# Experts: the second matrices are split in their own expert's opening step, and the sums of weight quarters move into the delta turns

## The chip, the cores and the metric

One core of a Trainium2 chip runs the whole program. The metric is the device time of one execution in microseconds. The kernel is written by hand: every engine has its own instruction stream, and semaphores alone order the streams.

## The reference, cut to what matters

The program is a stack of four layers on 4096 tokens of 256 values. The change touches the second layer, a mixture of eight experts, and the copies of weights that the fourth layer reads much later.

```python
# layer 2, on z = layernorm(x), after a delta-rule attention (layer 1)
probs = softmax(z @ w_router); weights = top-2 of probs, as a mask over 8 experts
h   = gelu(z @ w1[e] + b1[e])          # 256 -> 1024, for every expert e
out = sum over e of weights[:, e] * (h @ w2[e] + b2[e])   # 1024 -> 256
x   = x + out
# layer 4 has two 1024x1024 matrices, h1 and h2; the kernel multiplies them by blocks
# with seven products in place of eight, from sums of 512x512 quarters of each matrix
```

## The kernel before, in words

**The delta turns.** Layer 1 works through the 4096 tokens in 16 turns of two chunks (`TURNS`). Behind the turns, in pieces spread over them, follow the residual sum (x1), the layernorm z1 of it, the router and, for each block of four chunks, the place of every token in its two experts' lists. GpSimd (POOL) has three jobs here. For each chunk of a turn it multiplies one tile (L384) and issues the load of a word block `ckb` (L373), which VectorE folds into `lowb` (L622). Between turns it issues the scatters of z1 rows into `z1_by_expert` (L344): 64 indirect DMAs in all, eight to each block, half a block per pass of its loop over `u`. The order of that loop is written out by hand: `turn(u + 1)` first, then the scatters of pass u. The last six scatters stand in the next program block (L1529).

SyncE (SP) stores the finished tokens of each block (L294) and, behind the first five stores, issues 14 copies of weight quarters from the input to `hidden_weight_blocks` (L297), 1024 KB each, three to a block. These are the first terms of the sums that layer 4 needs. At the end SP loads the first expert's matrices (L313, L314).

**The experts.** The tokens of an expert are worked on in tiles of 256 (`TT`); this input gives 35 tiles. A step has TensorE (PE) make the up product of tile t (`up`, L1468 to L1470 through the helper `mm3`), transpose the rows of the next tile (L1597), and make the down product of the tile before (`down`). ScalarE (ACT) takes each of eight up results from its PSUM bank with the gelu (L1666); four banks are used in turn, so PE can be four of them ahead. VectorE (DVE) splits h into a high and a low part (L1760, L1762), adds the bias to the down result (`y`, L1728), and ACT multiplies it by the gate (`gated`, L1655) before POOL adds the rows to the tokens in DRAM (L1542).

Every product is made of three in a rounded format, so each weight matrix is needed as a high part (ACT, `high_part`, L1658) and a low part (DVE, `low_part`, L1743), and there are two buffers of either. The step that opens an expert (`before < e`) makes the up product of its first tile and the down product of the last tile of the expert before. In that step ACT makes the high part of the next expert's first matrix, waits for the end of the down product (`dn_ps`) and makes the high part of the next expert's second matrix; only then comes `gated`. DVE makes the low part of the next first matrix ahead of `y`, and that of the next second matrix at the end of the step. SP loads both raw matrices two experts ahead (`weights`, L1495, L1496).

**The sums of quarters** are made by POOL in the experts' openings (`hidden_sums`, L1551): 16 DMAs of 512 KB with `accum_op=add` into `hidden_weight_blocks`, two behind the token additions of each of the openings 1 to 5 and three in each of 6 and 7. In opening 7 POOL goes on with two multiplications of the next layer's weights (L1534).

Of the kernel before, what the change touches and what calls it, by code (L numbers as in the profile page):

```python
# [16 lines left out]
S, D, DS, HID, NE = 4096, 256, 64, 1024, 8  # L17
# [11 lines left out]
NP7 = 7  # L29
# [47 lines left out]
def build(nc, A):  # L77
# [5 lines left out]
    with ctx:  # L83
# [4 lines left out]
        first_sems = []  # L88
# [171 lines left out]
        hw_cp, hw_add = sem("hidden_blocks_copied"), sem("hidden_blocks_summed")  # L260
        first_terms = ((W_A11, 0, 0), (W_A12, 0, 1), (W_A22, 1, 1), (W_S3, 0, 0), (W_S1, 1, 1), (W_S2, 0, 0), (W_S4, 0, 1))
        ew_ld, v_ld = sem("expert_weights_loaded"), sem("vectors_loaded")
        nw_ld = [sem(f"next_weights_loaded_{q}") for q in range(2)]
        x_rdy, lq_rdy, mk_cp = sem1("right_side_ready"), sem1("decayed_q_ready"), sem1("decay_rows_ready")
        mk_rdy, mk_ps, mk_out = sem1("masks_ready"), sem1("mask_transposes_in_psum"), sem1("masks_taken")

# [9 lines left out]
        @block.sync  # L276
        def _(sp):
            for n in range(XL):
                cs = slice(XP[n], XP[n + 1])
                sp.dma_start(x_tok[:, cs, :], x_tok_d[:, cs, :]).then_inc(ld_x[n], 16)  # L280
            sp.dma_start(vec[:, 0:11, :], A["vectors"].rearrange("p (n k) -> p n k", k=KT)).then_inc(v_ld, 16)
            sp.wait_ge(nu_out, NB)
            kept = ((0, 2 * D * HID), (WORDS - D * HID, WORDS))
            for lo, hi in kept:
                sp.dma_start(raw_d[lo:hi], A["ffn"][lo:hi]).then_inc(bulk, 16)
            sp.wait_ge(consts, 2)
            for d_, a0, a1 in fills:
                v = d_.rearrange("(a p r) d -> a p (r d)", p=128, r=4)
                for a in range(a0, a1):
                    sp.dma_start(v[a], zero[:, 0:v.shape[2]]).then_inc(bulk, 16)  # L290

            def store_tokens(b):
                sp.wait_ge(x1_rdy, 2 * b + 2)
                sp.dma_start(x2_blocks[b], x_tok[:, b * CPB:(b + 1) * CPB, :]).then_inc(x1_st, 16)  # L294

            def first_term(layer, i, out_half, in_half):
                sp.dma_start(hw_rows[layer * NP7 + i], quarter(layer, out_half, in_half)).then_inc(hw_cp, 16)  # L297

            terms = [(layer, *term) for term in first_terms for layer in range(2)]
            for b in range(NB - 3):  # L300
                store_tokens(b)
                for term in terms[3 * b:3 * b + 3]:
                    first_term(*term)
            free = x_tok[:, :, :].rearrange("p c d -> p (c d)")
            sp.wait_ge(x1_st, 16 * (NB - 3))
            sp.wait_ge(z1_rdy, 2 * (NB - 4))
            sp.dma_start(free[:, 0:KT * HID].rearrange("p (k n) -> p k n", k=KT),
                         A["w1"].rearrange("e (k p) n -> e p k n", p=128)[1]).then_inc(nw_ld[1], 16)
            sp.dma_start(free[:, KT * HID:KT * HID + HID // 128 * D].rearrange("p (k n) -> p k n", n=D),
                         A["w2"].rearrange("e (k p) n -> e p k n", p=128)[1]).then_inc(nw_ld[1], 16)  # L310
            store_tokens(NB - 3)
            sp.wait_ge(pp_ps, NC)
            sp.dma_start(st1[:, :, :], A["w1"].rearrange("e (k p) n -> e p k n", p=128)[0]).then_inc(ew_ld, 16)  # L313
            sp.dma_start(st2[:, :, :], A["w2"].rearrange("e (k p) n -> e p k n", p=128)[0]).then_inc(ew_ld, 16)  # L314
            for b in range(NB - 2, NB):
                store_tokens(b)
# [31 lines left out]
        def _(pool):  # L348
# [29 lines left out]
            def turn(t):  # L378
                for j in range(2):
# [6 lines left out]
                    if c + 2 < NC:  # L386
                        load_words(c + 2, j)

            turn(0)
            for u in range(2 * NB + 5):  # L390
                if u + 1 < TURNS:
                    turn(u + 1)
                b = block_of(u, 1, 7)
                if b == 0:
                    pool.wait_ge(bulk, BULK)
                if b is not None:
                    scatter(pool, b, 0, CPB)
                b = block_of(u, 0, 8)
                if b is not None and b < NB - 1:
                    scatter(pool, b, CPB, 2 * CPB)  # L400
# [1040 lines left out]

        def landed(e):

            return nw_ld[e % 2], 32 * ((e + 1) // 2)


        ptwo = ctx.enter_context(ExitStack())
# [40 lines left out]
        def _(sp):  # L1488
            sp.dma_start(b1s[:, :], A["b1T"]).then_inc(eb_ld, 16)

            def weights(e):
                if e >= 2:
                    sp.wait_ge(ew_rdy, e - 1)
                    sp.wait_ge(w2_rdy, e - 1)
                sp.dma_start(raw1[e % 2][:, :, :], w1_d[e]).then_inc(nw_ld[e % 2], 16)  # L1495
                sp.dma_start(raw2[e % 2][:, :, :], w2_d[e]).then_inc(nw_ld[e % 2], 16)  # L1496

            def rows(e, t0, i):
                sp.wait_ge(xt_ps, t0 + i + 1)
# [5 lines left out]
            for e in range(NE):  # L1505
                t0 = sp.value_load(tiles0[0:1, e:e + 1], min_val=MIN_TILES * e, max_val=MT - MIN_TILES * (NE - e))
                own = sp.value_load(own0[0:1, e:e + 1], min_val=MIN_TILES, max_val=S // TT)
                rows(e, t0, 0)
                if e == 0:
                    for n in range(NE):  # L1510
                        sp.dma_start(b2s[:, n, :], A["b2"][n:n + 1, :].broadcast_to([128, D])).then_inc(b2_ld, 16)
                    sp.wait_ge(x1_st, 16 * NB)
                if 1 <= e < NE - 2:
                    weights(e + 2)
                if e == 2:
                    sp.dma_start(wst, A["W_tm"].rearrange("(k p) n -> p k n", p=128)).then_inc(wt_ld, 16)
                    sp.dma_start(tmr_, A["tm"].rearrange("(o n) -> o n", o=1).broadcast_to([128, 3 * D])).then_inc(wt_ld, 16)
                with sp.Fori(1, own) as i:
                    rows(e, t0, i)
            total = tile_count(sp)  # L1520

            sp.wait_ge(xt_ps, total + 1)
# [3 lines left out]
        def _(pool):  # L1526
# [15 lines left out]
                    pool.indirect_dma_start(x2_d, bass.IndirectOffsetOnAxis(to_row[:, j:j + 1].bitcast(u32), 0), yg[:, j, :], None,  # L1542
                                            compute_op=ALU.add).then_inc(y_out, 16)

            def hidden_sums(n):

                def add(layer, to, half, more=None):
                    base = layer * NP7
                    source = quarter(layer, 1, 0) if more is None else hw_rows[base + more]
                    k = 2 * half  # L1550
                    pool.dma_start(hw_rows[base + to][:, k:k + 2, :], source[:, k:k + 2, :], accum_op=ALU.add).then_inc(hw_add, 16)  # L1551

                if n == 0:
                    pool.wait_ge(hw_cp, 16 * 2 * NP7)
                for half in range(2):
                    if n < 4:
                        add(n % 2, (W_S3, W_S1)[n // 2], half)
                    elif n < 6:
                        pool.wait_ge(hw_add, 16 * 8)
                        add(n % 2, W_S2, half, W_S1)  # L1560
                if n == 5:
                    pool.wait_ge(hw_add, 16 * 10)
                    add(0, W_S4, 0, W_S2)
                if n == 6:
                    pool.wait_ge(hw_add, 16 * 13)
                    add(0, W_S4, 1, W_S2)
                    for half in range(2):
                        add(1, W_S4, half, W_S2)

            def step(e, t, before, start):  # L1570
                add_to_tokens(t)
                if before < e and e >= 1:
                    hidden_sums(e - 1)
                if before < e and e == NE - 1:
                    time_mix_weights()

# [63 lines left out]
        @block.scalar  # L1640
        def _(act):
            act.sem_inc(h_act, 4)
            for done in first_sems:
                act.sem_clear(done)
            act.wait_ge(ew_ld, 32)
            for st_, w in ((st1, w1s[0]), (st2, w2s[0])):
                nc.scalar.activation(w[0][:, :, :], st_[:, :, :], ACT.Copy).then_inc(wh_rdy, 1)
# [12 lines left out]
            def step(e, t, before, start):  # L1660
                ahead = before < e and e + 1 < NE
                for m in range(KH):
# [5 lines left out]
                    if start and m == 5:  # L1668
                        act.wait_ge(ew_rdy, 1)
                        act.wait_ge(w2_rdy, 1)  # L1670
                        act.dma_start(st1[:, :, :], w1_d[2]).then_inc(nw_ld[0], 16)
                        act.dma_start(st2[:, :, :], w2_d[2]).then_inc(nw_ld[0], 16)
                if ahead:
                    act.wait_ge(*landed(e + 1))
                    high_part(w1s, raw1, e + 1)
                    act.wait_ge(dn_ps, t * 2 + 2)
                    high_part(w2s, raw2, e + 1)
                if not start:
                    gated(t)

# [9 lines left out]
        def _(dve):  # L1690
# [54 lines left out]
            def step(e, t, before, start):  # L1745
# [3 lines left out]
                for m in range(0, KH, 2):  # L1749
                    i = m // 2  # L1750
                    dve.wait_ge(h_act, t * KH + (m + 2 + 4))
                    if i < 3:
                        dve.wait_ge(hs_free, t * 3 + (i + 1))
                    else:
                        if ahead:
                            low_part(w1s, raw1, e + 1, 2 * e + 3, ew_rdy)
                        if not start:
                            y(before, t)
                        dve.wait_ge(dn_ps, t * 2 + 2)
                    V.tensor_copy(hs[0][:, m:m + 2, :], h32[:, m:m + 2, :]).then_inc(h_st, 1)  # L1760
                    dve.wait_ge(h_st, t * 4 + (i + 1))
# [2 lines left out]
                rows_of_tokens(t)  # L1764
                hand_on(t)
                if ahead:
                    low_part(w2s, raw2, e + 1, 2 * e + 4, w2_rdy)

            rows_split(0)
            dve.wait_ge(wh_rdy, 2)  # L1770
# [1669 lines left out]
```

## Time and profile before

| what | value |
|---|---|
| median of 3 runs | 2003.12 us (1997.04 to 2003.94) |
| profiled execution | 2002.26 us, of which the span from first to last instruction is 2000.2 us |
| mean granted TensorE clock | 0.957 of full |
| TensorE matmul busy | 1826.2 us (91%) |
| VectorE busy | 1479.8 us (74%) |
| ScalarE busy | 1113.1 us (56%) |
| GpSimd busy | 308.5 us (15%) |

The program has stages with different limits, so the shares above say little about one of them. Times in the views are microseconds from the start of the span. The delta turns end at about 463 us, the rest of the router's work to 516 us, the experts from 523 to 953 us, and the two last layers behind that.

### The profile page before, as it was taken

The page shows a single profiled execution, that of the slowest core. Times are in us where ns is not written, and L with a number is a line of the kernel's source. Part 1 is how long each engine was busy: PE and PEld are TensorE (multiplying, and loading weights), DVE is VectorE, ACT ScalarE, POOL GpSimd, SP SyncE. Part 2 cuts the span into 40 slices and gives each one's busy share as a digit, 9 for nine tenths or more (in the row PEclk, how much of TensorE's full clock was granted, in tenths as well). Part 3 has the DMA queues.
Part 4 walks back from the last instruction along what each step waited for, and adds up shares of the span by engine and source line. Part 5 has one row for each costly group of instructions (what it writes and reads, how often), then busy time and mean ns, then how long its engine had stood idle before and what let it go on. Part 6 is the DMA issues. An engine that isn't in the chain of part 4 may idle for free. (4 is left out here: it accounts for less than half of the span.)

```text
span 2000.2 us, 31208 instructions
## 1 busy us (share of the span) xinstructions
PE 1826.2 (91%) x10840; PEld 1561.7 (78%) x10840; DVE 1479.8 (74%) x2966; ACT 1113.1 (56%) x1987; POOL 308.5 (15%) x282
## 2 busy tenths in 40 slices
PE   7999999997499999999577769899999999999999
PEld 5688888886499999999455547677788888888887
DVE  7567888887576676666599889888776776776675
ACT  3656666663344443442688867664556456456454
POOL 0000012224333322333100011111000000000000
PEclk9999999996699999999888879999999999999999
DMA  3099334423446545344444553333343143142141
GB/s 110 29 393 405 128 120 141 142 92 117 128 96 136 112 88 111 64 75 69 128 112 87 108 128 136 144 126 127 116 142 132 54 176 128 56 176 106 58 174 64
DMA packets 107986, 251.79 MB, mean 126 GB/s; under 512 B 8992, under 2 KB 51616, under 8 KB 99616
## 3 DMA queue, kind: packets, MB, share of 16 engines
q1 hardware_dynamic: 82288, 201.16, 28.6%
q0 software_dynamic: 23680, 46.28, 12.6%
q10 hardware_dynamic: 1888, 2.67, 0.4%
q8 instruction: 75, 1.23, 0.3%
q14 instruction: 55, 0.45, 0.1%
HBM read 172.88 MB, written 107.61 MB: 140 GB/s over the span
## 5 line engine op out<-in xcount | busy, mean ns | idle before, releaser
L1542 POOL DMA_INDIRECT tokens_behind_spare_rows<-yg,row_of_token x70 | 119.1, 1701 | 294.9 <-DVE row_of_token L1733 273.2
L1666 ACT ACTIVATE h<-bank,b1s 128x256 f32<-128x256 f32 x280 | 123.6, 471 | 35.0 <-PE bank L1470 20.3
L3177 ACT ACTIVATE hidden_quarter<-hidden_quarter,scl 128x512 f32<-128x512 f32 x96 | 67.6, 721 | 118.8 <-DVE hidden_quarter L3013 118.7
L1655 ACT ACTIVATE yg<-yt,own_gates 128x256 f32<-128x256 f32 x68 | 31.0, 502 | 183.3 <-DVE yt L1728 176.9
L1223 PE MATMUL bank<-st,L 128*128 128x128 f32 x768 | 117.4, 279 | 13.2 <-DVE st L573 13.1
L957 ACT ACTIVATE L<-bank 128x512 f32<-128x512 f32 x128 | 75.1, 593 | 94.6 <-PE bank L1215 94.3
L2398 PE MATMUL bank<-split_0h,hidden_weights 128*128 128x512 f32 x320 | 126.5, 395 | 0.0
L2398 PE MATMUL bank<-split_1h,hidden_weights 128*128 128x512 f32 x320 | 125.4, 392 | 0.1
L2399 PE MATMUL bank<-split_0l,hidden_weights 128*128 128x512 f32 x320 | 125.3, 391 | 0.0
L2399 PE MATMUL bank<-split_1l,hidden_weights 128*128 128x512 f32 x320 | 125.3, 391 | 0.0
L1215 PE MATMUL bank<-L 128*128 128x128 f32 x640 | 119.3, 276 | 0.0
L1223 PEld LDWEIGHTS bank<-st,L 128*128 128x128 f32 x768 | 100.6, 193 | 17.7 <-DVE st L573 7.0
L573 DVE TENSOR_TENSOR st<-st,bank 128x256 f32<-128x256 f32 x192 | 75.0, 416 | 53.0 <-PE bank L1223 52.2
L1214 PE MATMUL bank<-L 128*128 128x128 f32 x512 | 101.4, 280 | 0.7
L2398 PE MATMUL bank<-split_2h,hidden_weights 128*128 128x512 f32 x256 | 101.4, 396 | 0.0
L1762 DVE TENSOR_TENSOR hsl<-h,hsh 128x512 fp32r<-128x512 f32 x140 | 96.9, 692 | 4.8
L2399 PE MATMUL bank<-split_2l,hidden_weights 128*128 128x512 f32 x256 | 100.2, 391 | 0.0
L1215 PEld LDWEIGHTS bank<-L 128*128 128x128 f32 x640 | 95.5, 194 | 0.0
L2965 DVE SCALAR_TENSOR_TENSOR hidden_quarter<-bank,scl,x_tok 128x512 f32<-128x512 f32 x64 | 47.4, 748 | 55.8 <-ACT x_tok L3140 55.8
L1468 PE MATMUL bank<-xTh,w_1h 128*128 128x256 f32 x288 | 81.2, 282 | 7.2 <-ACT h L1666 7.2
L2972 DVE TENSOR_TENSOR split_2l<-hidden_quarter,split_2h 128x1024 fp32r<-128x1024 f32 x48 | 59.1, 1251 | 35.4 <-ACT split_2h L3159 35.4
L1214 PEld LDWEIGHTS bank<-L 128*128 128x128 f32 x512 | 79.3, 194 | 7.2 <-issue 2.7
(488 smaller groups left out, 6013.6 us busy)
## 6 DMA issues: line engine op xcount, KB each, us to landing
hidden_weights<-hidden_weight_blocks SPq DMA_DIRECT2D x64, 1024.0 KB, 4.8
z_by_expert<-zero SPq DMA_DIRECT2D x64, 520.0 KB, 15.6
hidden_weight_blocks<-in_ffn_dram SPq DMA_DIRECT2D x14, 1024.0 KB, 9.8
ckb<-in_ffn_dram POOLq DMA_DIRECT2D x32, 352.0 KB, 5.0
xg<-z_by_expert SPq DMA_DIRECT2D x36, 260.0 KB, 3.2
x_tok<-in_w_dram SPq DMA_DIRECT2D x8, 1024.0 KB, 8.8
x_tok<-x_T SPq DMA_DIRECT2D x16, 512.0 KB, 6.1
x_tok<-after_time_mix SPq DMA_DIRECT2D x15, 512.0 KB, 8.8
```

What stands on the lines that cost most here:

```text
L573: V.tensor_tensor(z_ if SQUARES <= n < LEVELS - 1 else x_, x_, B[2 + j][:, 0:256], ALU.subtract if n == 0 else ALU.add).then_inc(ap_rdy, 1)
L957: A_.activation(L[:, p, j, (n + 1) % 2, :, :], src, ACT.Copy).then_inc(sq_cp, 1)
L1214: T.matmul(B[j][:, 256 * m:256 * m + 128], b_, a, start=True, stop=True)
L1215: last = T.matmul(B[j][:, 256 * m + 128:256 * m + 256], a, b_, start=True, stop=True)
L1223: last = T.matmul(B[2 + j][:, 0:256].rearrange("p (a m d) -> p a m d", a=2, m=2)[:, :, m, :], Ln[:, 2 * m + 1, :], right, start=True, stop ...
L1468: nc.tensor.matmul(out, a[0], b[0], start=first, stop=False)
L1542: pool.indirect_dma_start(x2_d, bass.IndirectOffsetOnAxis(to_row[:, j:j + 1].bitcast(u32), 0), yg[:, j, :], None, compute_op=ALU.add).then ...
L1666: nc.scalar.activation(h32[:, m, :], B[m % 4][:, 0:TT], ACT.Gelu_apprx_tanh, bias=b1s[:, e * KH + m:e * KH + m + 1]).then_inc(h_act, 1)
L1762: V.tensor_tensor(hs[1][:, m:m + 2, :], h32[:, m:m + 2, :], f32(hs[0][:, m:m + 2, :]), ALU.subtract).then_inc(h_rdy, 1)
L2398: nc.tensor.matmul(out, w, x[0], start=first, stop=False, **more)
L2399: return nc.tensor.matmul(out, w, x[1], start=False, stop=last, **more)
L3177: A_.activation(QB[to][:, m, :], src, ACT.Gelu, scale=scl[:, off[lay.name] + row:off[lay.name] + row + 1]).then_inc(g_act, 1)
```

## The change

Five edits, as the diff has them:

1. The second matrix of expert e is split in opening e and no longer in opening e-1 (ACT `high_part(w2s, raw2, e)` ahead of that of the next first matrix, no wait for `dn_ps`; DVE `low_part(w2s, ...)` behind `y`). The low part of the next first matrix goes to the end of DVE's step.
2. So `y` stands ahead of both low parts in an opening.
3. The raw second matrices get semaphores of their own, and SP loads them one expert later than the first matrices.
4. `hidden_sums` leaves the experts. It becomes four groups of four DMAs in POOL's passes u = 12 to 15 of the delta turns, each between `turn(u + 1)` and the pass's scatters. The first group waits for all 14 copies, each later one for the landing of all the groups before it. SP issues the copies five to a block instead of three.
5. The clearing of the first stage's semaphores goes from the start of ACT's expert program to the end of SP's loops.

```diff
@@ first program block, SP @@
-                for term in terms[3 * b:3 * b + 3]:
+                for term in terms[5 * b:5 * b + 5]:
                     first_term(*term)
...
-                         A["w2"].rearrange("e (k p) n -> e p k n", p=128)[1]).then_inc(nw_ld[1], 16)
+                         A["w2"].rearrange("e (k p) n -> e p k n", p=128)[1]).then_inc(nd_ld[1], 16)
@@ first program block, POOL @@
+            def hidden_sums(n):
+                if n == 0:
+                    pool.wait_ge(hw_cp, 16 * 2 * NP7)
+                else:
+                    pool.wait_ge(hw_add, 16 * 4 * n)
+                to, more = ((W_S3, None), (W_S1, None), (W_S2, W_S1), (W_S4, W_S2))[n]
+                for layer in range(2):
+                    source = quarter(layer, 1, 0) if more is None else hw_rows[layer * NP7 + more]
+                    for k in (0, 2):
+                        pool.dma_start(hw_rows[layer * NP7 + to][:, k:k + 2, :], source[:, k:k + 2, :],
+                                       accum_op=ALU.add).then_inc(hw_add, 16)
+
             turn(0)
             for u in range(2 * NB + 5):
                 if u + 1 < TURNS:
                     turn(u + 1)
+                if 0 <= u - (TURNS - 4) < 4:
+                    hidden_sums(u - (TURNS - 4))
@@ experts, SP @@
-            def weights(e):
-                if e >= 2:
-                    sp.wait_ge(ew_rdy, e - 1)
-                    sp.wait_ge(w2_rdy, e - 1)
+            def up_weights(e):
+                sp.wait_ge(ew_rdy, e - 1)
                 sp.dma_start(raw1[e % 2][:, :, :], w1_d[e]).then_inc(nw_ld[e % 2], 16)
-                sp.dma_start(raw2[e % 2][:, :, :], w2_d[e]).then_inc(nw_ld[e % 2], 16)
+
+            def down_weights(e):
+                sp.wait_ge(w2_rdy, e - 1)
+                sp.dma_start(raw2[e % 2][:, :, :], w2_d[e]).then_inc(nd_ld[e % 2], 16)
...
+                if 2 <= e < NE - 1:
+                    down_weights(e + 1)
                 if 1 <= e < NE - 2:
-                    weights(e + 2)
+                    up_weights(e + 2)
...
+            for done in first_sems:
+                sp.sem_clear(done)
@@ experts, POOL @@
-            def hidden_sums(n):
...
             def step(e, t, before, start):
                 add_to_tokens(t)
-                if before < e and e >= 1:
-                    hidden_sums(e - 1)
                 if before < e and e == NE - 1:
                     time_mix_weights()
@@ experts, ACT @@
             act.sem_inc(h_act, 4)
-            for done in first_sems:
-                act.sem_clear(done)
...
+                if before < e and e >= 1:
+                    act.wait_ge(*down_landed(e))
+                    high_part(w2s, raw2, e)
                 if ahead:
                     act.wait_ge(*landed(e + 1))
                     high_part(w1s, raw1, e + 1)
-                    act.wait_ge(dn_ps, t * 2 + 2)
-                    high_part(w2s, raw2, e + 1)
                 if not start:
                     gated(t)
@@ experts, DVE @@
                     else:
-                        if ahead:
-                            low_part(w1s, raw1, e + 1, 2 * e + 3, ew_rdy)
                         if not start:
                             y(before, t)
+                        if before < e and e >= 1:
+                            low_part(w2s, raw2, e, 2 * e + 2, w2_rdy)
                         dve.wait_ge(dn_ps, t * 2 + 2)
...
                 hand_on(t)
                 if ahead:
-                    low_part(w2s, raw2, e + 1, 2 * e + 4, w2_rdy)
+                    low_part(w1s, raw1, e + 1, 2 * e + 3, ew_rdy)
```

## Rows read from the trace of the kernel before

**Rows 1.** The page: TensorE's busy tenths and clock, 40 slices of 50 us

```profile
PE   7999999997499999999577769899999999999999
...
PEclk9999999996699999999888879999999999999999
```

**Rows 2.** Waits, 490 to 965 us: us in total, times, longest

```profile
PE bank L1597 <- DMA xg<-z_by_expert: 19.6, 2, 19.2
...
PE bank L1468 <- ACT h L1666: 12.1, 8, 3.2
```

**Rows 3.** Timeline of PE after gaps: start, us, line, tile, count, idle before

```profile
523.05 1.12 PE L1597 MATMUL bank<-ident,xg 128*128 128x128 f32 x4 [19.20 <-DMA xg<-z_by_expert]
...
552.32 0.38 PE L1468 MATMUL bank<-xTh,w_0h 128*128 128x256 f32 x1 [0.88 <-ACT h L1666]
588.75 0.38 PE L1468 MATMUL bank<-xTh,w_1h 128*128 128x256 f32 x1 [1.34 <-ACT h L1666]
...
924.48 0.58 PE L1468 MATMUL bank<-xTh,w_1h 128*128 128x256 f32 x1 [3.16 <-ACT h L1666]
```

**Rows 4.** Timeline of ACT in expert 1's opening

```profile
584.71 1.93 ACT L1658 ACTIVATE w_0h<-st 128x2048 fp32r<-128x2048 f32 x1 [3.80 <-PE bank L1470]
587.43 0.91 ACT L1655 ACTIVATE yg<-yt,own_gates 128x256 f32<-128x256 f32 x2 [0.80 <-DVE yt L1728]
```

**Rows 5.** Timeline of DVE in the same opening

```profile
584.37 2.28 DVE L1743 TENSOR_TENSOR w_0l<-st,w_0h 128x2048 fp32r<-128x2048 f32 x1
586.57 0.75 DVE L1728 TENSOR_TENSOR yt<-bank,b2s 128x256 f32<-128x256 f32 x2
...
588.64 2.28 DVE L1743 TENSOR_TENSOR w_0l<-st,w_0h 128x2048 fp32r<-128x2048 f32 x1
```

**Rows 6.** Timelines of POOL and DVE in expert 7's opening

```profile
914.04 5.18 POOL L1534 TENSOR_TENSOR x_tok<-x_tok 128x768 f32<-128x768 f32 x2
...
915.08 4.45 DVE L1760 CAST hsh<-h 128x512 fp32r<-128x512 f32 x1
```

**Rows 7.** Timeline of POOL around the last delta turns

```profile
415.86 0.58 POOL L373 DMA_DIRECT2D ckb<-in_ffn_dram  x1 [16.15 <-DVE lowb L622]
...
440.11 0.58 POOL L373 DMA_DIRECT2D ckb<-in_ffn_dram  x1 [16.26 <-DVE lowb L622]
441.00 1.02 POOL L344 DMA_INDIRECT z_by_expert<-Z,slotz  x1 [0.30 <-issue]
...
463.53 0.97 POOL L344 DMA_INDIRECT z_by_expert<-Z,slotz  x1 [0.30 <-issue]
483.00 0.97 POOL L344 DMA_INDIRECT z_by_expert<-Z,slotz  x1 [18.49 <-DVE slotz L733]
...
516.27 0.97 POOL L344 DMA_INDIRECT z_by_expert<-Z,slotz  x1 [0.30 <-issue]
```

**Rows 8.** Sums by line, openings 1 and 6: duration (ns), start, landing

```profile
L1551 POOL DMA_DIRECT2D hidden_weight_blocks<-in_ffn_dram x2: 1955/2152/2348, 593.6 to 594.4; - x2
DMA to landing us min/median/max: 8.8/9.7/10.5
...
L1551 POOL DMA_DIRECT2D hidden_weight_blocks<-hidden_weight_blocks x3: 1481/1752/2199, 868.0 to 869.2; - x3
DMA to landing us min/median/max: 7.7/10.0/13.8
```

**Rows 9.** Stretches: busy us of PE, PEld, DVE, ACT, POOL; clock, DMA share, GB/s

```profile
868.00:884.00 16.00, 16.00 (x140) 16.00 (x140) 11.10 (x27) 4.44 (x10) 6.55 (x6) 1.00 0.98 159
...
426.00:440.00 14.00, 13.00 (x112) 12.19 (x108) 11.10 (x37) 8.69 (x25) 0.00 (x0) 1.00 0.11 39
...
471.00:480.00 9.00, 3.43 (x14) 2.42 (x14) 8.27 (x26) 2.58 (x5) 0.00 (x0) 0.50 0.88 291
```

**Rows 10.** Timelines of DVE and of PE in the last delta turn

```profile
442.85 0.88 DVE L622 TENSOR_TENSOR lowb<-lowb,ckb 128x704 int32<-128x704 int32 x1
...
463.72 0.77 PE L1247 MATMUL bank<-state,st 128*128 128x128 f32 x2 [1.07 <-DVE Wb L580]
```

More of the change, by code:

```diff
@@ L262, in build @@
         ew_ld, v_ld = sem("expert_weights_loaded"), sem("vectors_loaded")
-        nw_ld = [sem(f"next_weights_loaded_{q}") for q in range(2)]
+        nw_ld = [sem(f"next_up_weights_loaded_{q}") for q in range(2)]
+        nd_ld = [sem(f"next_down_weights_loaded_{q}") for q in range(2)]
         x_rdy, lq_rdy, mk_cp = sem1("right_side_ready"), sem1("decayed_q_ready"), sem1("decay_rows_ready")
@@ L1442, in landed, with down_landed @@
         def landed(e):
-            return nw_ld[e % 2], 32 * ((e + 1) // 2)
+            return nw_ld[e % 2], 16 * ((e + 1) // 2)
+        def down_landed(e):
+            return nd_ld[e % 2], 16 * ((e + 1) // 2)
         ptwo = ctx.enter_context(ExitStack())
@@ L1543, in add_to_tokens @@
                                             compute_op=ALU.add).then_inc(y_out, 16)
-            def hidden_sums(n):
[L1547 to L1568, printed above, removed]
             def step(e, t, before, start):
                 add_to_tokens(t)
-                if before < e and e >= 1:
-                    hidden_sums(e - 1)
                 if before < e and e == NE - 1:
@@ L1671, in step @@
                         act.dma_start(st1[:, :, :], w1_d[2]).then_inc(nw_ld[0], 16)
-                        act.dma_start(st2[:, :, :], w2_d[2]).then_inc(nw_ld[0], 16)
+                        act.dma_start(st2[:, :, :], w2_d[2]).then_inc(nd_ld[0], 16)
+                if before < e and e >= 1:
+                    act.wait_ge(*down_landed(e))
+                    high_part(w2s, raw2, e)
                 if ahead:
```

## The prediction

> **What bounds the kernel now.** I read the page's slices first. In the experts (slices 10 to 18) PE is busy all the time, and the clock is full after the start; ahead of them stands a stretch with PE at 4 tenths and a lower clock [rows 1]. The reader should take from this that the experts are bound by PE, so that an edit there is worth only the holes in PE's time, and that the way into the experts is bound by something else. The waits of the window name both: PE waits 19.2 us at once for the rows of the first tile, and 12.1 us in 8 pieces for the gelu to free a bank [rows 2]. PE's own timeline puts the pieces in their places [rows 3]: 0.88 us behind the first step, 1.34 us behind opening 1 (and 1.34 or 1.35 behind each of openings 2 to 6: six holes), and 3.16 us behind opening 7.
>
> **Why the holes are there.** In opening 1 the down product ends by 584.7. Only then does ACT make the high part of the second matrix, 1.93 us, and it waits 0.80 more for the bias addition [rows 4]; DVE is in a low part of 2.28 us from 584.37, so its addition starts at 586.57 instead of 584.7 [rows 5]. The gating comes 2 us late, the gelu behind it too, and PE, four banks ahead, runs out of banks. In opening 7 there is nothing to split. There a cast of DVE takes 4.45 us, and it ends only after POOL's two multiplications [rows 6].
>
> **What bounds the way in.** POOL's timeline [rows 7]: scatters follow one another every 1.275 us (0.97 busy, 0.30 idle). There are 8 to each block; three eights stand between 483.00 and the last one at 516.27, which waited for no places. The idle time of 18.49 us ahead of 483.00 is POOL's slack. PE begins at 523.05, 6.8 us after the last scatter's start [rows 3, 7]: the scatter, its landing and the load of the rows. Every microsecond by which the last scatter is late is paid in full.
>
> **The change part by part.** The sum stands against the profiled execution, 2002.26 us (span 2000.2 and 2.1 around it); the median of the runs is 0.9 above that.
>
> *Splits and bias addition in the opening.* The work is the same: 7 high parts of 1.93 and 7 low parts of 2.28 [rows 4, 5], one opening later. In openings 1 to 6 ACT now makes two high parts behind the eighth gelu, which ended 3.80 + 1.93 us ahead of 584.71 [rows 4]: from 579.0 to 582.9, before the down product ends. The addition starts at 584.7, the gating ends some 2 us after that, and a bank is free when PE wants it, as in any other tile. That takes away 6 x 1.34 = 8.0. The first step loses one high and one low part, and with them its 0.88. What is late next is DVE: behind the addition come 2.28, a cast and subtraction, and 2.28 again, which makes 584.7 + 0.75 + 2.28 + 1.1 + 0.3 + 2.28 = 591.4. PE came to a stop at 588.75 - 1.34 = 587.4, in the middle of an up product begun at 584.5 [rows 3], so without the stop it has the next rows transposed by 590.8; DVE's lateness runs down over the next tile's splits, and its addition is some 0.5 us late, of which I let PE pay 0.15. Six times, that is 0.9. The down product of the second tile needs the low part at about 590; it is made at 587.7. **Experts: -8.0.**
>
> *Opening 7.* It gains a high and a low part, both behind what PE waits for. POOL no longer has three sums ahead of its multiplications, so these come 1.7 us earlier and meet the tile's first DVE instructions instead of the cast. The lock-out lasts 5.2 us either way [rows 6]; I take 0, with bounds of -1 and +1.
>
> *Loads.* SP has one wait split in two; each second matrix is issued an expert ahead of its use, at least two tiles of 11.6 us or so (two halves of an up product are 5.8 and a down product as long), and even the 512 KB sums land in 8 to 14 [rows 8]. What is queued behind the new waits are the rows of the expert's second tile; both semaphores were raised an opening before, so 0. *Semaphore clearing* leaves ACT's start, where the path is the scatters', and goes to SP's end, ahead of a load that waits for PE anyway: 0. *Copies five to a block*: 14 copies by the third block, into DMA engines that stand at 0.11 in a quiet stretch [rows 9]; word blocks are loaded most of a turn ahead; SP only waits for x1 behind them: 0, with an upper bound of 1.
>
> *The sums in POOL's passes.* First their price. Two sums issued 0.8 us apart land within 0.8 + 10.5 = 11.3 us; three in opening 6 within 1.2 + 13.8 = 15.0, where two of that kind took 10.5, so a further one costs 4.5 [rows 8]. Four are 11.3 + 9.0 = 20.3 us for a group from the input, 19.5 for one inside the copy. During them the DMA engines are full (share 0.98), at 159 GB/s [rows 9]: they are bound by the engines, and nothing says they would be faster elsewhere. The issues of three take 1.2 us from the first start to the last and up to 2.2 for the last [rows 8], so 1.1 each, and 4.5 for four.
>
> By the Trainium skill, "DMA: Bandwidth & Descriptors", section "Anatomy of one DMA — SWDGE (gpsimd) path", such a transfer takes about 2.0 us and its bytes at 436 GB/s; that would be some 7 us for four (an estimate by that page), and the groups would not wait for each other. Its fit says nothing of accumulation, and the landings above disagree with it.
>
> Now the chain on POOL:
> - Group 0 follows the word block of 415.86 [rows 7], at 416.7, and lands at 437. The next word block is issued behind it and behind four scatters, at 416.7 + 4.5 + 5.1 + 0.5 = 427, and must be there at 442.85 [rows 10]; it comes behind the group and the scatters in the queue, at about 440. 0, at worst 3.
> - Group 1 follows the word block of 440.11, at 441.0 [rows 7], and lands at 441.0 + 20.3 + 1 for that block = 462.3. The half block of scatters behind it and the last two multiplications of the turns end at 441.0 + 4.5 + 5.1 + 1 = 452; PE wants these at 463.7 [rows 10]. 0.
> - Group 2 must wait for group 1: 462.3. Alone it would land at 481.8. But from 471 to 480 SP loads the first expert's 2 MB and stores a block, a share of 0.88 over 9 us, 7.9 us of all engines [rows 9]. Full engines mean the two add up: 489.7.
> - Group 3 waits for that: 489.7, and is issued by 494.2. Behind it stand the scatters of blocks 4 to 7, 32 in all, 31 x 1.275 = 39.5: the last starts at 533.7, and not at 516.3 [rows 7]. The last block had its places without a wait by then [rows 7], so nothing else is later than POOL.
>
> **Way into the experts: +17.4**, between +9.5 (the loads overlap with group 2 at no cost: 481.8) and, with 5.2 us a further sum, the word block late by 3 and a queue that holds scatters up, about +28.
>
> For the adding up of group 2 and the loads there is a rule beside the rows: the same page, section "Queues, rings and completion order", says that each DMA engine takes the queues in turn, packet by packet. By it the engines do both works one after the other, as taken above.
>
> *Sum.* 2002.3 - 8.0 + 17.4 = **2011.7, say 2011**, 8 above the median of the runs. About 0.5%, or 10 us, is what a measurement of this kernel can tell from no change, so this is on the slow side of no change, and near the edge.
>
> **The rivals.**
> - *Slower: POOL's chain is longer than worked out.* Place: group 3 and the 32 scatters behind it. Price: from 4.5 to 5.2 us for a further sum in four groups, of which three are on the chain, +4 to +6, and the queue's hold on the scatters while group 3 lands (until about 510), a few more: +25 in all, and 2019. It decides against me when group 3 is issued later than 492. For it: every small delay on the chain adds to the others. Against it: in opening 6 three sums were taken by the queue at once [rows 8].
> - *Faster: the sums are not the price.* By the page's figure, or if the quiet DMA engines of these turns do four sums in under 10 us, group 2 is done at 462 and group 3 at 472, the scatters of 483 are on time, and only -8.0 is left: 1994. For it: POOL's slack of 18.49 us. Against: landings and share [rows 8, 9].
> - *The holes stay.* If DVE's double load in the opening makes the next tile late by as much as was gained, the change does not do what it says, and only +17.4 stands: 2019.7. Against it: the addition is first in line when the down product ends.
> - *The loads cost group 2 nothing*: -8.0 + 9.5, 2004.
>
> **How the numbers follow.** The forecast's own case, chain and gain as worked out, has 0.48 and a spread of some 4 us about 2011, from 2007 to 2015. The longer chain has 0.22 (2015 to 2024), the holes that stay 0.06, the free loads 0.14 (2001 to 2007), cheap sums 0.10 (1993 to 1996). Left out of the range are cheap sums and the far end of the longer chain. Range 1999 to 2022. Against the median of 2003.1 the edges of no change are 1993 and 2013. Slower takes a third of the first case (0.16) and all of the next two (0.28): 0.44. Faster has 0.05: half of the cheap sums. The same: 0.51.
>
> **What would show it.** Right: the pieces of 1.34 us behind openings 1 to 6 are gone from PE's timeline; the wait of PE for the first rows is about 36 us and not 19.2, and PE begins the experts at about 540; POOL has no slack ahead of its last 32 scatters; one issue of group 2 comes at about 462, one of group 3 at about 490; the expert stage from its first to its last product is 8 us shorter. Wrong: group 3 issued before 476, so that POOL catches up; or a hole of DVE's making in the second tile of each expert; or a wait for a word block at 443, which would move the turns themselves.

## The result and the profile after

The changed kernel takes 1992.25 us (median of 5 runs, 1989.26 to 1997.32) against 2003.94 us for the kernel before in the same session: a ratio of 0.9949 with a 95% interval of 0.9928 to 0.997. Timed twice more on other occasions it gave 0.9965 (0.9951 to 0.9979) and 0.9947 (0.993 to 0.9963). It is faster by about half a per cent, and the forecast was 0.4% slower. The profiled execution is 1992.25 us long, its span 1990.5.

PE's timeline of the changed kernel, the lines with idle time ahead of them, answers to [rows 2, 3]:

```profile
524.17 1.12 PE L1594 MATMUL bank<-ident,xg 128*128 128x128 f32 x4 [23.75 <-DMA xg<-z_by_expert]
526.95 0.57 PE L1487 MATMUL bank<-xTh,w_0h 128*128 128x256 f32 x1 [1.67 <-DVE xTl L1716]
537.18 0.38 PE L1487 MATMUL bank<-xTh,w_0h 128*128 128x256 f32 x1 [1.66 <-DVE xTl L1716]
543.70 0.66 PE L1594 MATMUL bank<-ident,xg 128*128 128x128 f32 x4 [0.81 <-DMA xg<-z_by_expert]
914.88 0.58 PE L1487 MATMUL bank<-xTh,w_1h 128*128 128x256 f32 x1 [2.96 <-ACT h L1661]
```

Between 543.70 and 914.88 no hole is left: the 0.88 and the six of 1.34 us are gone. The 2.96 us behind opening 7 are still there (3.16 before). The wait for the first rows is 23.75 us, not the 36 that were forecast.

POOL's timeline, in answer to [rows 7]: the word block that ends the last turn but one, the sums of group 1, of group 2 and of group 3, and the first and last scatter behind them.

```profile
438.59 0.58 POOL L374 DMA_DIRECT2D ckb<-in_ffn_dram  x1 [12.13 <-DVE lowb L637]
439.16 4.76 POOL L399 DMA_DIRECT2D hidden_weight_blocks<-in_ffn_dram  x4
...
456.81 3.50 POOL L399 DMA_DIRECT2D hidden_weight_blocks<-hidden_weight_blocks  x4 [6.71 <-DMA hidden_weight_blocks<-in_ffn_dram]
...
472.79 3.50 POOL L399 DMA_DIRECT2D hidden_weight_blocks<-hidden_weight_blocks  x4 [7.24 <-DMA hidden_weight_blocks<-hidden_weight_blocks]
...
476.59 1.04 POOL L345 DMA_INDIRECT z_by_expert<-Z,slotz  x1 [0.31 <-issue]
...
517.35 0.97 POOL L345 DMA_INDIRECT z_by_expert<-Z,slotz  x1 [0.30 <-issue]
```

The chain is the one forecast: POOL waits for group 1 and for group 2 (the two waits on a DMA), and from 476.59 on it has no slack. But group 3 comes at 472.8, where 489.7 was worked out.

**Where the 9.7 us of the two spans come from**, by the same event in both traces:

| event | before | changed | difference | of it in this stretch |
|---|---|---|---|---|
| PE's first instruction | 8.47 | 6.95 | -1.5 | -1.5 |
| SP's load of the first expert (end of the turns) | 471.13 | 467.05 | -4.1 | -2.6 |
| PE transposes the first rows | 523.05 | 524.17 | +1.1 | +5.2 |
| second step's first product | 536.27 | 537.18 | +0.9 | -0.2 |
| first product behind opening 7 | 924.48 | 914.88 | -9.6 | -10.5 |
| next layer's first transposes | 968.70 | 958.95 | -9.75 | -0.15 |

The first line is ahead of every edit. The second goes with the clock: PE's granted clock fell to half at about 463 us in the last turn of the kernel before, and at about 467 us in the changed one.

```profile
450.00:464.00 14.00, 11.52 (x96) 10.67 (x95) 11.50 (x41) 5.84 (x13) 9.26 (x10) 0.97 0.24 86
464.00:480.00 16.00, 9.88 (x39) 7.39 (x39) 12.11 (x46) 2.81 (x6) 0.50 (x1) 0.50 0.53 176
```

```profile
450.00:464.00 14.00, 11.57 (x98) 10.52 (x96) 11.41 (x42) 5.07 (x11) 6.38 (x8) 1.00 0.82 162
464.00:480.00 16.00, 7.97 (x36) 5.12 (x32) 14.07 (x60) 5.49 (x13) 7.55 (x9) 0.60 1.04 269
```

(Stretches of the kernel before, then of the changed one, columns as in [rows 9].) Another profiled execution of the same changed kernel began its first instruction at 8.41, had a mean clock of 0.78 from 460 to 465 us, and took 31.0 us from the word block to SP's load, where this one took 28.5 and the kernel before 31.0. So neither line belongs to the change. What is left to explain is the stretch on the way in, which costs, and the experts, which gain. The +5.2 of the third line is not all the change's: while POOL is the last to come, the 2.6 us by which the turns ended earlier are not used, and the chain itself adds the other 2.6.

### The profile page after: what moved, and what is told of

Same layout as the page of the kernel before. It is cut to its first block and busy times, and to the rows that moved or that the text cites. A ratio compares the mean times of both kernels' runs of the same rounds, so it can differ in the third digit from the quotient of the medians.

```text
span 1990.5 us, 31195 instructions
## 1 busy us (share of the span) xinstructions
PE 1821.0 (91%) x10840; PEld 1558.3 (78%) x10840; DVE 1476.9 (74%) x2966; ACT 1114.6 (56%) x1987; POOL 308.9 (16%) x282
## 5 line engine op out<-in xcount | busy, mean ns | idle before, releaser
L1712 DVE COPY raw_gates<-xg 128x8 f32<-128x8 f32 x36 | 8.0, 221 | 103.7 <-PE bank L1594 103.0
L1229 PEld LDWEIGHTS bank<-L 128*128 128x128 f32 x512 | 78.8, 193 | 7.3 <-issue 2.7
```

What stands on the lines that cost most here:

```text
L1229: T.matmul(B[j][:, 256 * m:256 * m + 128], b_, a, start=True, stop=True)
```

## The experiments

All kernels are compared by two stretches, which leave out the first accident and most of the second: **way in**, from the word block that ends the last turn but one to the last scatter (76.2 us before, 78.8 changed), and **experts**, from the second step's first product to the first one behind opening 7 (388.2 before, 377.7 changed). The way in isn't quite free of the clock. Where POOL has slack, it waits for the places that the turns deliver: one and the same kernel (early_apart and apart_again below) took 75.4 us with the turns' end 28.5 us behind the word block, and 76.8 us with 31.0. So differences of up to 1.4 us in the way in need not come from an edit.

**splits_only**: the changed kernel with the sums back in the openings.

```diff
-                if 0 <= u - (TURNS - 4) < 4:
-                    hidden_sums(u - (TURNS - 4))
...
-                for term in terms[5 * b:5 * b + 5]:
+                for term in terms[3 * b:3 * b + 3]:
...
                 add_to_tokens(t)
+                if before < e and e >= 1:
+                    hidden_sums(e - 1)
```

> The changed kernel with the sums of quarters back in the experts' openings and the copies three to a block: the edits of the splits alone. Theory A (the gain of the change is the closed holes of PE in the openings, and the sums play no part in the experts): from PE's first up product to the first product behind opening 7 the stage is as short as in the changed kernel, about 388 us and not 398.7; PE's holes behind openings 1 to 6 are gone; the way in is as in the kernel before, last scatter about 75 us after the first scatter of 441.0. Time some 10 us under the kernel before. Rival B (taking the sums out of the openings frees POOL and the DMA engines, and part of the gain comes from that): the expert stage gets back at least 3 us of its length, and holes or later bias additions are seen in openings with sums.

Measured: ratio 0.9969 (0.9958 to 0.9981). Way in 76.8 us, experts 380.7. So the splits alone are worth 7.5 us of the experts, and the sums' leaving is worth 3.0 more. Rival B has its part, and PE's timeline shows where:

```profile
877.35 0.38 PE L1473 MATMUL bank<-xTh,w_0h 128*128 128x256 f32 x1 [0.83 <-ACT h L1674]
917.64 0.58 PE L1473 MATMUL bank<-xTh,w_1h 128*128 128x256 f32 x1 [5.09 <-ACT h L1674]
```

Behind opening 6 a new hole of 0.83 us, and 5.09 in place of 2.96 behind opening 7. ACT's timeline names the first one's cause, and the landings of the token additions (issued from 860 to 872 us, splits_only, then the changed kernel) give its size:

```profile
876.03 0.91 ACT L1663 ACTIVATE yg<-yt,own_gates 128x256 f32<-128x256 f32 x2 [7.82 <-DMA tokens_behind_spare_rows<-yg,row_of_token]
...
DMA to landing us min/median/max: 4.2/9.3/9.3
```

```profile
DMA to landing us min/median/max: 3.7/3.8/4.4
```

The additions stand behind the three sums in POOL's queue and land after 9.3 us instead of 3.8; `gated` waits for them (`y_out`), and the gelu behind it. The second hole is the meeting of DVE and POOL in opening 7. Here two instructions of DVE are long and not one: a cast while POOL issues the sums, which ends at 907.45, and a subtraction across POOL's multiplications.

```profile
905.62 1.83 DVE L1769 CAST hsh<-h 128x512 fp32r<-128x512 f32 x1
907.48 5.64 DVE L1771 TENSOR_TENSOR hsl<-h,hsh 128x512 fp32r<-128x512 f32 x1
```

```profile
905.69 3.19 POOL L1561 DMA_DIRECT2D hidden_weight_blocks<-hidden_weight_blocks  x3
907.59 4.98 POOL L1544 TENSOR_TENSOR x_tok<-x_tok 128x768 f32<-128x768 f32 x2
```

Beside the 0.42 and 0.69 us that the two take elsewhere, DVE loses 6.36 us; in the changed kernel its one long cast (4.65 for 0.42) loses 4.23. The difference is 2.13, and so is that of the two holes (5.09 and 2.96).

**sums_only**: the kernel before with the sums moved (and the copies five to a block).

```diff
-                if before < e and e >= 1:
-                    hidden_sums(e - 1)
...
+                if 0 <= u - (TURNS - 4) < 4:
+                    hidden_sums(u - (TURNS - 4))
```

> The kernel before with the sums moved into passes 12 to 15 and the copies five to a block, and nothing else. Theory A: the six holes of 1.34 us stay, the expert stage keeps its 398.7 us, and the way in gets 2 to 4 us longer, because POOL waits for groups 1 and 2 (about 17 us a group) and then issues 32 scatters in a row. Time 1 to 5 us over the kernel before. Rival B: the expert stage is shorter by 3 us or more and the time is at or under that of the kernel before. My forecast's own price (20 us a group, 27 for the one beside the loads) would give 15 us more on the way in.

Measured: ratio 1.0004 (0.9992 to 1.0016). Way in 78.6 us, so +2.4 where the forecast had +17.4:

```profile
437.97 0.58 POOL L373 DMA_DIRECT2D ckb<-in_ffn_dram  x1 [12.14 <-DVE lowb L636]
...
471.63 3.49 POOL L398 DMA_DIRECT2D hidden_weight_blocks<-hidden_weight_blocks  x4 [7.76 <-DMA hidden_weight_blocks<-hidden_weight_blocks]
...
516.54 0.97 POOL L344 DMA_INDIRECT z_by_expert<-Z,slotz  x1 [0.30 <-issue]
```

Experts 387.6: the six holes of 1.34 stay, the first is 0.43 and that of opening 7 is 1.95. The sums' move alone is a little cost and a little gain, and the time cannot tell it from nothing.

**sums_early**: the groups three passes earlier, in 9 to 12.

```diff
-                if 0 <= u - (TURNS - 4) < 4:
-                    hidden_sums(u - (TURNS - 4))
+                if 0 <= u - (TURNS - 7) < 4:
+                    hidden_sums(u - (TURNS - 7))
```

> The changed kernel with its four groups in passes 9 to 12 instead of 12 to 15, so that a group has a turn of 23.7 us to itself and none stands ahead of the last 32 scatters. Theory A (the chain on POOL is what the sums cost): POOL waits for no landing, its slack ahead of the scatters of the fifth block is back at 10 us or more, PE's wait for the first rows is back to 19 to 20 us, and the time is 2 to 5 us under the changed kernel. Rival C (four sums in a turn cost the turns themselves, by late word blocks or by port time taken from DVE): the turns with a group are longer than 23.7 us by a microsecond or more, and the time is not under the changed kernel's.

Measured: ratio 0.9944 (0.9929 to 0.996). Way in 75.4 us, experts 377.6. POOL's slack is back:

```profile
478.28 0.97 POOL L345 DMA_INDIRECT z_by_expert<-Z,slotz  x1 [16.73 <-DVE slotz L748]
```

The last word blocks stand 23.4 and 24.3 us apart (389.47, 412.89, 437.15), as in the kernel before (392.44, 415.86, 440.11): in these turns a group costs nothing, and rival C falls.

**addition_first**: the kernel before, with the bias addition ahead of the first matrix's low part.

```diff
-                        if ahead:
-                            low_part(w1s, raw1, e + 1, 2 * e + 3, ew_rdy)
                         if not start:
                             y(before, t)
+                        if ahead:
+                            low_part(w1s, raw1, e + 1, 2 * e + 3, ew_rdy)
```

> The kernel before with one swap in DVE's opening step: the bias addition ahead of the low part of the first matrix. ACT still makes the high part of the second matrix behind the down product. Theory A (the hole of 1.34 us is set by the later of two chains, DVE's late addition until 587.3 and ACT's high part until 586.6): the holes shrink to about 0.55 us, and the rest goes only when ACT's high part moves too. Rival D (DVE's addition alone makes the hole): they go to 0. Rival E (ACT's high part alone): they stay at 1.34.

Measured (one execution, 1996.53 us): the six holes are 0.44 us each, and the experts take 382.9 us.

```profile
586.42 0.39 PE L1468 MATMUL bank<-xTh,w_1h 128*128 128x256 f32 x1 [0.44 <-ACT h L1666]
```

**low_part_first**: the changed kernel with the low part ahead of the addition.

```diff
-                        if not start:
-                            y(before, t)
                         if before < e and e >= 1:
                             low_part(w2s, raw2, e, 2 * e + 2, w2_rdy)
+                        if not start:
+                            y(before, t)
```

> The changed kernel with the low part of the second matrix ahead of the bias addition in DVE's opening step (ACT's early high part stays). Theory A (two chains make the old hole, DVE's late addition the longer one): the addition is 2.1 us late again and the holes behind openings 1 to 6 are back at 1.3 us or a little more, and one of like size joins the 2.96 us in opening 7. Rival E (ACT's high part alone made the hole): no holes.

Measured (one execution, 1998.03 us): holes of 1.34 to 1.35 us behind openings 1 to 6, and in opening 7 one of 1.35 ahead of one of 2.35. Experts 387.7. With addition_first this settles the hole's making: DVE's late addition alone makes all 1.34, and ACT's late high part alone 0.44 of it. Moving only one of them would have left a hole; the change moves both.

```profile
584.01 0.38 PE L1487 MATMUL bank<-xTh,w_1h 128*128 128x256 f32 x1 [1.35 <-ACT h L1661]
...
921.10 0.39 PE L1487 MATMUL bank<-xTh,w_1h 128*128 128x256 f32 x1 [2.35 <-ACT h L1661]
```

**group2_held**: the collision that the forecast had worked out, made on purpose.

```diff
                 else:
                     pool.wait_ge(hw_add, 16 * 4 * n)
+                if n == 2:
+                    pool.wait_ge(pp_ps, NC)
```

> The changed kernel with one more wait: group 2 also waits for the end of the last delta turn, at which SP issues the 2 MB of the first expert. So group 2 and the loads start together. Theory H (sums and loads add up on full DMA engines; the change escaped it because group 2 had landed 6 us after the loads began and the collision fell on group 3, which nobody waits for): group 2 takes 16 + 4 to 6 = 20 to 22 us from its first issue to the wait's end, and the last scatter comes 15 us or more later than in the changed kernel (10 for the later start, 5 for the collision). Rival I (they overlap at no cost): 14 to 16 us, and 10 us later.

Measured (one execution, 2003.95 us):

```profile
465.92 3.49 POOL L401 DMA_DIRECT2D hidden_weight_blocks<-hidden_weight_blocks  x4 [17.50 <-PE bank L1268]
484.55 0.95 POOL L401 DMA_DIRECT2D hidden_weight_blocks<-hidden_weight_blocks  x1 [9.90 <-DMA hidden_weight_blocks<-hidden_weight_blocks]
```

```profile
536.87 1.12 PE L1596 MATMUL bank<-ident,xg 128*128 128x128 f32 x4 [37.99 <-DMA xg<-z_by_expert]
```

Group 2 takes 18.6 us from issue to the end of the wait. In the changed kernel it took 16.0, in its two other profiled executions 15.1 and 14.7 (457.31 to 472.37, and 457.23 to 471.88). In sums_only and low_part_first it took 16.5 and 15.6. In all of these the loads had begun 1.6 to 5.7 us ahead of the group's end. So the collision seems real, in a single execution, and costs 2 to 4 us (18.6 against 14.7 to 16.5): half or less of the 7.9 charged, and below the 20 to 22 of theory H. The way in is 92.7 us, 13.9 more than in the changed kernel where theory H asked for 15 or more, and PE waits 37.99 us for its first rows: the chain decides as forecast once group 3 is issued late enough.

**early_apart**: sums_early with POOL's two multiplications in openings 6 and 7, one each.

```diff
-                for k in range(KT):
-                    nc.gpsimd.tensor_tensor(wst[:, k, :], wst[:, k, :], tmr_, ALU.mult).then_inc(p_st2, 1)
+                nc.gpsimd.tensor_tensor(wst[:, k, :], wst[:, k, :], tmr_, ALU.mult).then_inc(p_st2, 1)
...
-                if before < e and e == NE - 1:
-                    time_mix_weights()
+                if before < e and e >= NE - 2:
+                    time_mix_weights(e - (NE - 2))
```

> The kernel of sums_early with POOL's two multiplications taken apart: one in opening 6, one in opening 7. Theory F (a multiplication of 2.1 to 2.6 us locks DVE's cast out for its whole length, and only what exceeds the slack of about 1 to 2 us ahead of the bias addition becomes a hole): in place of one hole of 2.95 us with a fall of the clock behind it there are two of about 1 us and no fall of the clock; 2 us faster than sums_early. Rival G (an opening has no slack): two holes of 2 us or more, no gain.

Measured: ratio 0.9961 (0.9945 to 0.9977). PE's timeline has two holes, and the product behind the second takes 0.38 us and not the 0.58 of a fallen clock:

```profile
862.29 0.38 PE L1487 MATMUL bank<-xTh,w_0h 128*128 128x256 f32 x1 [1.87 <-ACT h L1660]
910.19 0.38 PE L1487 MATMUL bank<-xTh,w_1h 128*128 128x256 f32 x1 [1.16 <-ACT h L1660]
```

From there to the next layer's first transposes it is 42.5 us, against 44.5 in sums_early (952.72 - 910.19, 954.62 - 910.14). That looks like theory F's clock. The next run, changed_again, doesn't fit it: it has the whole hole of 2.95 us, no fall behind it, and 42.8 us for the same stretch (957.51 - 914.73). Here are the windows behind the hole, in the changed kernel's first execution and in changed_again:

```profile
914.00:917.00 3.00, 2.12 (x10) 2.12 (x11) 0.98 (x6) 2.28 (x7) 1.56 (x1) 0.57 0.01 3
```

```profile
914.00:917.00 3.00, 2.27 (x19) 2.27 (x20) 0.83 (x6) 2.72 (x7) 1.57 (x1) 1.00 0.01 3
```

The same kernel, the same hole, and 10 products in one and 19 in the other. But all thirteen traces together speak for theory F. Nine of them have a hole of 2.95 us or more behind opening 7, and in eight the clock falls to half behind it (changed_again is the ninth); in the four whose hole there is 2.35 us or less (low_part_first, sums_only, early_apart, apart_again) it stays at 1.00. With a fall the stretch takes 44.1 to 44.5 us, without one 42.5 to 43.2; in the changed kernel alone it is 44.1 and 42.8, so a fall costs about 1.3 us there. The idle time itself is no shorter with the multiplications apart: 1.87 + 1.16 = 3.03 us for 2.95. So they save the fall of the clock, and the times don't show so small a gain.

**changed_again**, **changed_third**, **early_again** and **apart_again** repeat three kernels, the last three timed together.

> The changed kernel once more, on the same chip and against the same runs of the kernel before as early_apart. Expected 0.995 of the kernel before, again with holes only behind opening 7, the last scatter 78 to 79 us after the word block that ends the last but one turn, and the clock's fall at the end of the turns somewhere between 462 and 470 us.

> The changed kernel beside sums_early on one chip. From the traces so far: last scatter 78 to 79 us after the word block that ends the last but one turn. Ratio to the kernel before 0.995 to 0.9965.

> sums_early once more, beside the changed kernel. If the 3.3 us of the shorter way in (75.4 us and not 78.8) count in full, its ratio lies 0.0015 under that of the changed kernel in the same call; if something in the turns gives them back, the two ratios are the same.

> early_apart once more. By the traces it is 1.8 us faster than sums_early behind opening 7 (no fall of the clock), which is 0.0009 of the time and likely less than the timing can tell; its first timing had runs with a wide spread.

| kernel | ratio | way in | experts |
|---|---|---|---|
| changed_again | 0.9965 (0.9951 to 0.9979) | 78.1 | 377.6 |
| changed_third | 0.9947 (0.993 to 0.9963) | 78.0 | 376.6 |
| early_again | 0.9956 (0.9943 to 0.9969) | 75.3 | 377.3 |
| apart_again | 0.9943 (0.9925 to 0.996) | 76.8 | 378.6 |

The stretches of one kernel repeat within 1.4 us. The way in is 78.0 to 78.8 us in the three traces of the changed kernel and 75.3 to 76.8 in the four with early sums, so the chain's cost, 1.2 to 3.5 us, is seen in every trace, but not in the times: timed together, changed_third and early_again come in the other order, within the intervals. Larger differences lie outside of both stretches. From the next layer's first transposes to the end, early_again took 1036.0 us, and sums_early and the changed kernel 1031.5 and 1031.6; from the first instruction to the word block sums_early took 428.6 us, early_again 431.4. No version was shown to beat the changed kernel.

## Why the prediction was wrong

**Experts, -8.0: right in place, too small.** The stretch is 10.5 us shorter. Of the term's steps: six holes of 1.34 and the one of 0.88, gone as said. A hole cost more than its idle time: in opening 1 the first product came 1.62 us behind the last one (587.13 to 588.75), where products otherwise start 0.11 us apart, so 1.51 and not 1.34 (the view counts idle time from the modelled end of the last product, 0.28 us behind its start); seven times the difference of 0.17 is 1.2. The 0.9 us charged for DVE's late additions in the second tile did not come: no hole is there. 8.0 + 0.9 + 1.2 + 0.2 from opening 7 makes 10.3; a longer wait for the rows of a tile (0.81 us at 543.70, 0.40 before) takes 0.4 off, and 0.6 of the 10.5 stay without a name. Where this gain was said to be the splits' alone, that failed: 3.0 of it need the sums gone from the openings, though in the kernel before, with the old order, their going is worth only 0.6.

**Way in, +17.4: the mechanism was right, its price far too high (2.6 measured).** The step that failed is the price of a group:

- *A further sum, 4.5 us.* I took it from opening 6, where the third sum landed 4.5 us behind the second one [rows 8]. In the same rows the second one landed 2.9 behind the first (7.7, and 0.6 + 10.0), and the pair of opening 1 said 2.5 (8.8, and 0.8 + 10.5). The pairs of openings 2 to 5, which I had not read, lie at 2.5 to 3.6. So I had taken the dearest spacing for all. Why the third was late is open: token additions had gone into the queue ahead of its landing, but so they had in opening 1. In the changed kernel group 1's four land 8.7 us after the first issue and 15.2 after the last, at 441.3:

```profile
L399 POOL DMA_DIRECT2D hidden_weight_blocks<-in_ffn_dram x4: 1280/1906/2577, 439.2 to 441.3; - x4
DMA to landing us min/median/max: 8.7/12.1/15.2
```

  So a further one is (441.3 + 15.2 - 439.2 - 8.7) / 3 = 2.9. Group 1 held POOL 17.6 us and not 21.3.
- *The loads on top of group 2, 7.9 us.* With cheaper groups this mostly fell away: the loads began at 467.05, and group 2 had landed at 472.8, 16.0 after its issue instead of 27.4. The collision seems to have moved on to group 3, whose sums took up to 18.5 us to land and for which nobody waits on the way in. Made on purpose it costs 2 to 4 us, so here full engines did not mean that the two works add up one to one. Here the rule of the Trainium skill (page "DMA: Bandwidth & Descriptors", section "Queues, rings and completion order"), that an engine takes the queues in turn, is not contradicted, but the sum that I drew from it is.
- *Issue of four sums*: 3.8 us (472.79 to 476.59) for 4.5. *The last 32 scatters*: 40.8 us for 39.5.

Together 3.7 + 11.4 + 0.7 - 1.3 = 14.5 us less than the 92.7 forecast from 441.0 to 533.7, and 78.2 were measured from 439.16 to 517.35 (group 1 also follows its word block by 0.57 us and not by 0.89, which is the rest of 17.4 - 2.6). The cost that is left, 2.6 us on the way in, is the one shown by sums_only (2.4) and taken back by sums_early.

The fit on the same page of the Trainium skill (section "Anatomy of one DMA — SWDGE (gpsimd) path": 2.0 us and the bytes at 436 GB/s), which I set against the rows, gives by estimate 3.2 us for a sum alone and 1.2 for a further one. The landings disagree with it still: 8.7 and 2.9.

**The other terms** at 0: the copies, the loads and the clearing left no wait in the trace. The word block behind group 0 was not late: the last turn keeps its length. Opening 7 had bounds of -1 and +1 and moved by -0.2.

**The rivals.** "The sums are not the price", with its 1994, was nearest, and group 3 was issued at 472.8 where it says 472. But its condition, four sums in under 10 us, was not met (17.6 and 16.0), POOL's slack was used up, and the way in did cost something; a gain of 10.5 in place of 8.0 made up for it, and 1.5 us of the profiled execution are its early start. So part of that nearness is luck. The sign "group 3 issued before 476, so that POOL catches up" came true in its first half only. "The holes stay" and "the chain is longer" did not happen.

## What to carry to other kernels

Price a queued transfer by all the spacings that the rows show, and put the spread into the range: here three spacings of 2.5, 2.9 and 4.5 us were at hand, and a chain of several groups multiplied the choice. Before a collision is charged to a step, ask whether the step is still there when the other work starts, with its cheap price as well as with its dear one. And where two engines both come late to the same point, a test that moves one of them shows only part of what both are worth: DVE alone took 0.90 off a hole of 1.34 us, ACT alone nothing, both all of it.

## What the runs showed of the hardware that was not expected

- A DMA behind accumulating ones in POOL's queue lands late: token additions 9.3 us after issue behind three sums of 512 KB, 3.8 without. Whether the queue's order or the full DMA engines (share 0.98 in [rows 9]) hold it was not tested.
- An instruction of DVE that meets POOL's two multiplications ends only after both, be it a copy, a cast or a subtraction (5.64 for 0.69 us in splits_only). A copy of 128x8 that takes 0.17 us took 3.70 in sums_only; in the changed kernel it was the cast:

```profile
913.77 3.70 DVE L1703 COPY raw_gates<-xg 128x8 f32<-128x8 f32 x1 [3.48 <-PE bank L1584]
```

```profile
904.98 4.65 DVE L1756 CAST hsh<-h 128x512 fp32r<-128x512 f32 x1
```

- Behind one and the same hole of 2.95 us the clock was granted at 0.57 in one execution of the changed kernel, 1.00 in another, and in a third 0.68. In thirteen traces it fell behind eight of nine holes of 2.95 us or more and behind none of the four of 2.35 or less; one profile would have shown neither.
- The fall of the clock at the end of the delta turns came at about 463, 464 and 467 us in three executions of the changed kernel. From the word block to the end of the turns these took 31.0, 29.7 and 28.5 us: a spread of 2.5, a quarter of what was to be measured here.
